# A third-half load moved ahead of w1, and two weight-scale sums and two transpose groups moved behind later products, in a conditioned ternary FFN kernel

## The reference

```python
q_emb = relu(q @ W3 + b3)                       # one 256-vector per batch
v_sum = sum(v, axis=1, keepdims=True)           # over the 32 steps
c = relu(((n * v + v_sum) * q_emb[:, None, :]) @ W2 + b2)      # v is x, n = 32
s = mean(abs(w)); w_q = clip(round(w / s), -1, 1) * s          # for each of w1, w3, w2
out = x + (silu(c @ w1q.T) * (c @ w3q.T)) @ w2q.T              # hidden size 682
```

## Time and profile before

| What | Value |
|---|---|
| Runs, median (lowest to highest) | 165.83 us (165.24 to 166.05) |
| The profiled execution, its own time | 165.95 us |
| Its span, first to last instruction | 164.2 us |
| Outside the span | 1.75 us |
| Mean granted TensorE clock | 1.0 of full |
| TensorE matmul busy | 159.7 us (97%) |
| VectorE, ScalarE, GpSimd busy | 116.4, 89.6, 55.1 us |
| DMA moved | 12.67 MB |

### The profile page before, as it was taken

One profiled execution on the slowest core, in us unless ns is written; L12 is line 12 of the kernel. 1 busy time (PEld: TensorE's weight loads), 2 busy tenths in 40 slices (PEclk: granted clock), 3 DMA queues, 4 the chain that ended last, 5 costly groups with the idle time before them and its releaser, 6 DMA issues.

```text
span 164.2 us, 2295 instructions
## 1 busy us (share of the span) xinstructions
PE 159.7 (97%) x764; PEld 131.1 (80%) x764; DVE 116.4 (71%) x187; ACT 89.6 (55%) x163; POOL 55.1 (34%) x53
## 2 busy tenths in 40 slices
PE   7999999999999999999999999999999999999992
PEld 4778787888887888788887888788887888788892
DVE  2566999978978891788548891888548870566863
ACT  4077888435844475345844466355744566255540
POOL 5014023402360276204841276204841266001500
PEclk9999999999999999999999999999999999999999
DMA  4997566665565589300250007000150006000063
GB/s 130 296 356 163 87 100 99 97 97 88 92 100 95 92 191 166 50 4 0 35 93 0 0 4 122 8 0 0 29 101 4 2 0 113 15 0 4 16 112 128
DMA packets 67412, 12.67 MB, mean 77 GB/s; under 512 B 63216, under 2 KB 67144, under 8 KB 67400
## 3 DMA queue, kind: packets, MB, share of 16 engines
q1 hardware_dynamic: 67248, 12.46, 38.7%
q10 hardware_dynamic: 152, 0.07, 0.1%
HBM read 8.32 MB, written 4.19 MB: 76 GB/s over the span
## 4 chain that ended last, share of the span: by engine, by line
PE 91%; DMA 4%; SPq 2%; issue 0%; DVE 0%
PE bank L538 49%; PE bank L581 21%; PE bank L469 15%; DMA xo<-in_x_dram 4%; PE bank L565 3%; PE bank L484 1%; PE bank L445 1%; SPq L212 1%; PE bank L496 0%; PE bank L478 0%; SPq L218 0%; SPq L217 0%; SPq L224 0%; SPq L216 0%; SPq L222 0%
## 5 line engine op out<-in xcount | busy, mean ns | idle before, releaser
L538 PE MATMUL bank<-c_hi,T 128*128 128x512 f32 (+1 forms) x176 | 69.2, 393 | 0.0
L538 PE MATMUL bank<-c_lo,T 128*128 128x512 f32 (+1 forms) x176 | 68.8, 391 | 0.0
L389 ACT ACTIVATE silu<-bank,checked 128x512 f32<-128x512 f32 (+1 forms) x48 | 33.1, 690 | 51.5 <-PE bank L538 51.3
L778 DVE SCALAR_TENSOR_TENSOR gf<-bank,out_scale,silu 128x512 f32<-128x512 f32 (+1 forms) x42 | 31.3, 744 | 34.7 <-PE bank L538 31.0
L538 PEld LDWEIGHTS bank<-c_hi,T 128*128 128x128 f32 (+1 forms) x176 | 32.8, 186 | 7.6 <-issue 0.2
L538 PEld LDWEIGHTS bank<-c_lo,T 128*128 128x128 f32 (+1 forms) x176 | 32.8, 186 | 7.3
L272 POOL TENSOR_TENSOR x<-y,qT 128x512 f32<-128x512 f32 x12 | 13.7, 1144 | 53.6 <-DVE y L685 53.6
L469 PE MATMUL bank<-x,W_sb 128*128 128x256 f32 x128 | 29.5, 381 | 0.4 <-DMA W_sb<-in_L_cond_W_dram 0.4
L581 PE MATMUL bank<-g_hi,T 128*128 128x512 f32 x70 | 28.5, 407 | 0.0
L786 DVE TENSOR_TENSOR g_lo<-gf,g_hi 128x512 fp32r<-128x512 f32 x40 | 28.5, 712 | 0.0
L581 PE MATMUL bank<-g_lo,T 128*128 128x512 f32 x70 | 27.3, 390 | 0.0
(11 more groups left out here) (78 smaller groups left out, 108.8 us busy)
## 6 DMA issues: line engine op xcount, KB each, us to landing
xb<-in_x_dram SPq DMA_DIRECT2D x64, 64.0 KB, 2.7
out_dram<-turned SPq DMA_DIRECT2D x28, 128.0 KB, 2.7
xo<-in_x_dram SPq DMA_DIRECT2D x3, 256.0 KB, 4.7
w_sb<-in_L_ffn_w_dram SPq DMA_DIRECT2D x2, 384.0 KB, 6.3
w_sb<-in_L_ffn_w_dram SPq DMA_DIRECT2D x1, 682.0 KB, 8.4
w_sb<-in_L_ffn_w_dram SPq DMA_DIRECT2D x2, 256.0 KB
xo<-in_x_dram SPq DMA_DIRECT2D x1, 512.0 KB, 4.9
xo<-in_x_dram SPq DMA_DIRECT2D x2, 128.0 KB, 2.5
```

Of the source, the lines that this page charges most:

```text
L389: nc.scalar.activation(silu[r, m % 2, :], h1[j % 2][r], ACT.Silu, scale=checked[r, 0:1]).then_inc(silu_done, 1)
L538: last = pe.matmul(dst[j % 2][0:w, :], T13[:, k, col:col + w], part[:, g % NC, k, :], start=(i == 0), stop=(i == len(passes) - 1))
L778: nc.vector.scalar_tensor_tensor(out=gf[r, m % 3, :], in0=second, scalar=out_scale[r], in1=silu[r, m % 2, :], op0=ALU.mult, op1=ALU.mult). ...
```

## The change

Four lists change. SyncE issues the load of the fourth half before w1 and not between w1 and w3. ScalarE does `relu(1)` between the two parts of w1's absolute sum. VectorE scales the fourth half before w1's threshold and not after the first part of w1 is above it. TensorE does `sum_partitions(0)` behind `project_c(2)`, `project_c(3)` ahead of w1's first transposes, w3's first transposes behind `h1_step(0)`, and `h1_step(1)` ahead of `h3_step(0)`.

```diff
             load_half(2)
+            load_half(3)
 
             sp.wait_ge(zeroed, 2)
             load_w13(w1_sb, w1, got_w1)
-            load_half(3)
             load_w13(w3_sb, w3, got_w3)
...
             relu(0)
             abs_sum(0, w1_sb, 0, got_w1[0], 16)
+            relu(1)
             abs_sum(0, w1_sb, 1, got_w1[1], 32)
-            relu(1)
             abs_sum(1, w3_sb, 0, got_w3[0], 16)
...
             mix_x(3)
+            project_c(2)
             pe.wait_ge(const_ready, 4)
             sum_partitions(0)
-            project_c(2)
+            project_c(3)
 
             pe.wait_ge(x1_done, EARLY - 1)
             transpose_w13(0, 0, w1_t)
 
             pe.wait_ge(q_ready, DC)
             sum_partitions(1)
-            project_c(3)
-            transpose_w13(1, 0, w3_t)
...
             h1_step(0)
+            transpose_w13(1, 0, w3_t)
+
+            h1_step(1)
             pe.wait_ge(relu_done, DC * HALVES)
             pe.wait_ge(T3_copied, 1)
             h3_step(0)
             transpose_w13(0, 1, w1_t)
-
-            h1_step(1)
             transpose_w13(1, 1, w3_t)
...
             early_lo(0)
+            scale_mixed(3)
             limit(0)
             above_limit(0, w1_sb, w1_t, parts[0])
-            scale_mixed(3)
             limit(1)
```

## The result

| | before | after |
|---|---|---|
| Median, runs of one series (12 and 12) | 165.80 us (165.08 to 166.24) | 166.63 us (165.97 to 166.90) |
| Profiled execution, its span | 165.95, 164.2 us | 166.69, 164.9 us |

The ratio is 1.0044 with a 95% interval of 1.0029 to 1.0060: slower by 0.7 us (0.5 to 1.0), beyond what the runs scatter, and just within the half per cent that the prediction called no change.

A forecast was written before the change was run, and what follows sets the result against it. TensorE, its matmuls busy for 159.7 of 164.2 us, was taken as the bound; -0.21, -0.21, +0.07, +0.76 and +0.30 gave +0.71, and 165.83 + 0.70 a median of 166.5 us, range 165.9 to 167.2.

The forecast's parts named there:

- The gap ahead of the first product: TensorE idles from 16.35 to 17.11 ahead of the first product with c, waiting for w1's signs: +0.76 us.
- VectorE's late part of w2's sum: VectorE's chain starts later with w3's sum, so TensorE waits at w2's sum: +0.30 us, bounds 0 and 0.45.
- The load: Issued ahead of w1, the fourth half lets its mix start at 11.11, not 11.32: -0.21 us, bounds 0 and 0.21.
- The wait of w3's sum: The wait of w3's sum behind the four transposes, for ScalarE's last sum, goes away: -0.21 us.
- w1's sum: On TensorE w1's sum costs 0.21 between two products and cost 0.14 before: +0.07 us.
- Covered costs: w1's later landing and VectorE's earlier scaling cost nothing; swapping h1_step(1) and h3_step(0) just hides w3's signs, 0.05 to spare.
- Rival 1: The lag grows: TensorE also waits at h1_step(2) and the next two steps, 0.3 to 0.6 us more, 167.0; 12%.
- Rival 3: The load of the fourth half lands no sooner, every start is 0.21 later: +0.9 us, 166.7; 7%.
- Rivals 2 and 4: 2: order is free, only the wins stay, -0.35, 165.5, 8%; 4: the clock falls in the new gap, 169.3, 3%.

The follow-up runs named there:

- cover: The changed kernel with the second half of the fourth product with W2 moved behind w3's sum, over w1's signs; 166.05 against 165.82 us, ratio 1.0017.
- sum_back: The changed kernel with w1's sum back ahead of the third product and relu(1) back behind both parts of w1's absolute sum; 166.69 us, ratio 1.0059.
- before_again: The kernel before, unchanged, profiled once more; one run, 166.42 us.
- b_only: The kernel before with only w1's sum, the fourth product, relu(1) and scale_mixed(3) moved as in the change; 166.83 us, ratio 1.0057.
- c_only: The kernel before with only w3's first transposes behind h1_step(0) and h1_step(1) ahead of h3_step(0); 165.66 against 165.66 us, ratio 0.9995.
- no_load: The changed kernel without the moved load: the fourth half is loaded behind w1 again; 166.70 us, ratio 1.0053.
- late_sum: The kernel before with w3's sum inside the fourth product, w3's first transposes behind h1_step(0), h1_step(1) ahead of h3_step(0); 165.93 against 165.91 us, ratio 0.9996.
- after_again: The changed kernel, unchanged, profiled once more; one run, 165.98 us.
- tile_first: The changed kernel with the signs of w1's first tile in an instruction of their own, h1_step(0) waiting for that one alone; ratio 1.0041.
- a_load: The kernel before with only the load of the fourth half moved ahead of w1; 165.78 against 165.66 us, ratio 0.9997.
- late_sum_load: The same lists as late_sum, with the fourth half also loaded ahead of w1; 166.01 against 165.91 us, ratio 1.0011.

## Why the prediction was right, and where it was not

- **Size and sign.** Forecast +0.70 us, measured +0.83 between the medians and 0.5 to 1.0 by the ratio. In the profiles the distance grew by 0.48 us, 0.13 came behind it, and the mix started 0.10 later. TensorE's list sets the end, and what it loses ahead of 22 us arrives at the end: the rest is 143.1 to 143.4 us in fourteen profiles.
- **The gap ahead of the first product, +0.76.** From w3's sum to the product it is 0.89 us, less the 0.21 that a sum costs: 0.68. The place is as forecast, and the length lies between the bounds of 0.62 and 0.9; that w1's signs end it is read from the 0.09 us between their end and the product, as the profile names no releaser. cover takes the gap away and sum_back shows what it does not depend on.
- **VectorE's late part of w2's sum, +0.30.** The mechanism holds, the size was too large: 0.12. Counted from the mix, VectorE's part of w2 was forecast to end at 21.32 - 11.11 = 10.21 us and ended at 21.23 - 11.42 = 9.81; TensorE was forecast to be free at 10.05 and was at 9.80 (20.32 + 0.90 - 11.42). VectorE gained more, mainly because the tiles above w3's threshold took 0.75 us and not 0.89 once GpSimd was idle beside them. The prediction's lower bound allowed for a gain of this kind, but on the tiles of 2.48 us, which took 2.47.
- **The load, -0.21.** This term was read from one execution and has no fixed size. In before_again, b_only, c_only, no_load and late_sum the fourth half stood between w1 and w3 as before, and TensorE came to the mix at 11.38 or later without a wait, so there was nothing to win. In after_again and tile_first, with the load moved, it came at 10.71 without a wait, 0.6 us ahead of the mix of before, and the distance stayed 10.14 and 10.12: there the gain survived. How much it is on average is open: the changed lists gave a ratio of 1.0044 with it and 1.0053 without it (after, no_load), and the old lists 0.9997 with it (a_load), and their intervals overlap. Nor does the old place always mean a landing at 11.3: the fastest of the runs of no_load had a span of 163.9 us, which with a distance of 10.13 and a rest of 143.2 puts its mix at about 10.6, an estimate.
- **The wait of w3's sum, -0.21, and w1's sum, +0.07.** The first is gone (0.23 us from transposes to sum, and not 0.41). w1's sum costs 0.14 where it stands now too, so the second is 0.
- **What was left out.** A mix that has not waited costs 0.89 to the next step and not 1.00, a product behind it 1.73 and not 1.81. Their weight loads run ahead: in the changed kernel the mix's first load is at 11.21, 0.21 before its first matmul, and the product's at 12.21, 0.10 before; in the kernel before, behind the wait, load and matmul of the mix both start at 11.32. By such items the distance was forecast as 21.67 - 11.11 = 10.56 us and measured 10.13. That the total came out right all the same is partly luck, as three errors cancel in the profiled execution: 0.43 too much in the distance, 0.31 too little for the start of the mix (11.42 and not 11.11), and nothing for the wait of `h1_step(5)`, 0.13.
- **Covered costs.** w1's later landing, VectorE's scaling and the swap of the two products cost nothing in the profile, as said: w3's signs are between 18.56 and 19.16, and `h3_step(0)` starts at 19.34 with no idle time before it.
- **Rival 1** came, small and in another place. `h1_step(2)` did not wait: it starts at 22.56, and VectorE's first hidden product ended at 21.49 + 0.68 = 22.17. But VectorE stays late. It ends the weights of w2 above their threshold at 22.34 + 2.04 = 24.38, 2.83 us behind `h3_step(1)`, where before it was 21.41 + 1.64 = 23.05, 2.08 behind; then `h1_step(5)` waits for it. The fourteen profiles fall into two groups. In eight (after, after_again, no_load, sum_back, cover, tile_first, late_sum, late_sum_load) that end comes 2.81 to 2.84 us behind `h3_step(1)`, `h1_step(5)` waits, and the first product with w2's signs starts 8.53 to 8.57 behind it. In the other six they are 2.07 to 2.51 and 8.44 or 8.45, with no such wait. So 0.09 to 0.13 us belong to VectorE's late chain, where the prediction, with the same lists from there on, put nothing.
- **Rival 3** did not come in after_again and tile_first, where the half was there by 10.71; in the profiled execution TensorE came at 11.42 and could not tell.
- **Rivals 2 and 4** did not come. In the stretch from 16.0 to 17.2 with its gap the granted clock stayed at full, but this figure alone proves little, as it is 1.00 too in the kernel before from 0.90 to 3.30 us, over the first five matmuls of 512 columns, 0.46 us each (the second of the rows below). The spacing decides: behind the gap the matmuls start at 17.42, 17.66 and 17.89, 0.23 to 0.24 apart, as before the change.

```profile
16.00:17.20 1.20, 0.64 (x8) 0.58 (x7) 0.57 (x2) 0.78 (x2) 0.00 (x0) 1.00 0.62 99
```

```profile
0.90:3.30 2.40, 2.31 (x6) 0.90 (x7) 0.81 (x7) 1.29 (x2) 1.93 (x8) 1.00 0.49 149
```

## What to carry to other kernels

On an engine that is busy throughout, read each piece of work for what it covers on the others: the fourth product was worth its place because it lay over 0.64 us of signs and 1 us of VectorE, and moved ahead of the transposes it covered nothing. Shortening one gate shows nothing while a second one behind it hangs on something else; find what stands ahead of both. An engine that a change makes late can hold the others up long after the place of the change: here VectorE did at 29 us, and a wait of 0.1 us there is seen only if the same step is compared in all profiles. Before two profiles are subtracted, find a point behind which both run alike, and compare distances from there: here the start scattered by 1.1 us, more than the effect.

## What the runs showed of the hardware

- The moment at which TensorE's early matmuls become fast differs from execution to execution: the first mix took from 0.76 to 1.17 us in the fourteen profiles, from a start at 3.52 in twelve of them, and the mix of the fourth half started between 10.71 and 11.78. The granted clock is 1.00 from 3.50 to 4.70 us in before and after alike, where this mix took 0.76 and 1.17, so it doesn't show this.
- VectorE's instruction on the tiles above a threshold, which reads two operands from SBUF, waits for an instruction of GpSimd that runs beside it. The two tiles above w3's threshold in a_load, with GpSimd's subtraction over them:

```profile
14.41 1.27 POOL L291 TENSOR_TENSOR c_lo<-ct,c_hi 128x512 fp32r<-128x512 f32 x1 [1.29 <-DVE x L656]
```

```profile
14.89 1.34 DVE L716 SCALAR_TENSOR_TENSOR w_t<-size,limits,w_sb 128x512 bf16<-128x512 f32 x1
```

It takes 0.75 us alone (changed kernel, 16.85). Here GpSimd ends 0.79 us behind its start and it takes 0.59 more. In the kernel before, GpSimd ended 0.34 behind its start and it took 0.14 more (0.89). The reverse is in sum_back: there VectorE's tiles (13.64 to 14.39) began first, and the same subtraction of GpSimd, started at 13.76, took 1.76 us and not 1.27. The Trainium skill, "SBUF — State Buffer", section "SBUF: two separate sides", says that these two engines share a pair of ports: a VectorE instruction with two inputs in SBUF and a GpSimd one that reads SBUF exclude each other, whichever starts first has the pair for the whole instruction, and the other blocks. Both extras of VectorE are what was left of GpSimd's instruction less 0.20, which agrees.
